# Attention and top-2 experts on one core: expert choice on logits, shorter routing, work moved between engines, row maxima 24 steps ahead

## The chip, the cores and the metric

The kernel runs on 1 core of a Trainium2 chip. The metric is device time in microseconds, the median of several runs. Kernel before: 1321.52 us, median of 3 runs (1320.3 to 1324.97).

## What is computed

x is 16 sequences of 512 tokens of 128 numbers, fp32. Attention has 16 heads of 8; V and U (8 x 32) work inside each head, and a softmax over 512 keys lies between. Then a layer norm, a layer of 8 experts of which each token uses two, and a second layer norm.

```python
zq, zk, zv = q @ V, k @ V, v @ V
att = softmax(einsum('bhqr,bhkr->bhqk', zq, zk) / sqrt(32))
x = layernorm(x + (att @ zv @ U.T) @ Wo.T + bo)
p = softmax(x @ gate_w.T)            # 8 experts
scores, idx = top_k(p, 2);  scores /= scores.sum()
out = sum over the two of score_e * (relu(x @ w1[e].T + b1[e]) @ w2[e].T + b2[e])
x = layernorm(x + out)
```

## The kernel before

**Attention, batch by batch.** A batch is one sequence. `schedule` writes out one body for each n from -2 to 17 on every engine, so that five stages overlap: while batch b has its softmax (`cur`), batch b+1 has its row maxima (`nxt`), batch b+2 is projected and split (`proj`), batch b-1 is finished up to its gate logits (`prev`), and batch b-2 gets its experts chosen, its places computed and its rows scattered (`prev2`). A body has 32 steps s. In a step TensorE (PE) makes one score tile for the exponentials (`scores`, L578, two matmuls), one for the maxima (`maxima`, L594), after every second step one product with the values (`av`, L556), and then what `misc(s)` asks for: every odd step may use the one spare PSUM bank `misc_ps`. ScalarE (ACT) takes the exponential of a 128 x 1024 tile (L687), VectorE (DVE) the maximum over such a tile (L853). Three PSUM tiles `score_ps` go round: `scores(s)` waits for the maximum of step s-2 (`red_done`), `maxima(s)` for the exponential of step s-1 (`exp_done`).

**Row maxima.** The negated maxima are needed in transposed form as extra rows of `q_stack`. After each 16 steps of maxima PE transposes them (`max_transpose`, at s = 23 for half 0 of b+1 and at s = 1 for half 1 of b), DVE negates (`neg`, L700, at s = 24 and 2), GpSimd (POOL) splits the fp32 numbers into three bf16 parts (`split_max`, four instructions), and SP issues six small DMAs (`max_rows`, L944), on which `scores(0)` and `scores(16)` wait.

**Expert choice.** For batch b-1 the logits appear at s = 27. `choose` is a chain of 21 small DVE instructions (k = 0 to 20), each waiting for the one ahead of it: it subtracts the largest logit, ACT takes the exponential (s = 30), and the softmax is finished before the two largest probabilities are found. k = 0 to 3 run at s = 28 and 31, the others in the first nine steps of the next body. PE counts the tokens of each expert at s = 17, `route` (k = 0 to 8, ten instructions) turns that into row numbers at s = 18 to 22, and POOL starts eight indirect DMAs (L923), one for each of 4 token tiles and 2 choices, in one run at the end of its body, behind `split_max(n1, 0)`.

**Queues.** POOL's order in a body: split_max(b,1), x + bias (L902), split_q, 1/sqrt of the variance (L908, L911), split_k, split_max(b+1,0), eight scatters. SP's order: x_in, last stack group of b+1, x_res, max_rows(b,1), store q parts, store k parts, max_rows(b+1,0), then stack groups 0, 1, 2 of b+2 (L956, 256 KB each).

**Start and end.** In body -1 there are 32 steps of maxima alone; from s = 16 on, every second step also transposes one expert's weights, which have been loaded into `probs`. After the last batch come the tail of its chain and then the expert stage (136 tiles of 128 rows, L1088 to L1236) and the second layer norm; the change touches neither.

Of the kernel before, what the change touches and what calls it, by code (L numbers as in the profile page):

```python
# [17 lines left out]
HALF = STEPS  # L18
POS = 8
# [7 lines left out]
TOP_STEPS = 19  # L27
# [8 lines left out]
SCALE_AT = 18  # L36
# [35 lines left out]
def build_layer(nc, x, wq, bq, wk, bk, wv, bv, wo, bo, u, v, gate_w, w1, b1, w2, b2, out):  # L72
# [19 lines left out]
    with top:  # L92
# [13 lines left out]
        bv_b = sb("bv_b", [P, P])  # L106
# [16 lines left out]
        with att:  # L123
# [31 lines left out]
            rstd = asb("rstd", [P, QT])  # L155
            shift = asb("shift", [P, QT])

            rows = [[asb(f"rows{n}_{w}", [P, QT, ROW]) for w in range(2)] for n in range(2)]
# [5 lines left out]
            top_logit = asb("top_logit", [P, QT])  # L164
            logits = asb("logits", [P, QT, E])
            exps = asb("exps", [P, QT, E])
            gate_sum = asb("gate_sum", [P, QT])
            gate_inv = asb("gate_inv", [P, QT])
            gate_p = asb("gate_p", [P, QT, E])
# [5 lines left out]
            chosen = [[asb(f"chosen{n}_{w}", [P, QT, E]) for w in range(2)] for n in range(2)]  # L175
            pair_sum = asb("pair_sum", [P, QT])
            pair_inv = asb("pair_inv", [P, QT])
            chosen_any = [asb(f"chosen_any{n}", [P, QT, E], bf16) for n in range(2)]
            slot = asb("slot", [P, QT, E])
            slot_of = asb("slot_of", [P, QT, E])  # L180
            slot_f = asb("slot_f", [P, 2, QT])
            slot_i = [asb(f"slot_i{n}", [P, 2, QT], i32) for n in range(2)]
            place_i = asb("place_i", [P, 2, QT], i32)
            place_f = asb("place_f", [P, 2, QT])
# [27 lines left out]
            bv_wide = asb("bv_wide", [P, P])  # L212

# [13 lines left out]
            pe_setup, dve_setup, place_ready = sem("pe_setup"), sem("dve_setup"), sem("place_ready")  # L227

            with nc.Block() as block:
# [28 lines left out]
                def _(pool):  # L258
# [40 lines left out]
                    nc.gpsimd.iota(place_i[:, :, :], pattern=[[1, 2], [2 * P, QT]], base=0, channel_multiplier=2).then_inc(place_ready, 1)  # L299
# [3 lines left out]
                def _(pe):  # L303
# [3 lines left out]
                    for n in range(2):  # L307
# [18 lines left out]
                    nc.tensor.matmul(score_ps[2][:, 0, P:2 * P], bv_wide[:, :], vhr, start=True, stop=True).then_inc(pe_setup, 1)  # L326
                    pe.wait_ge(dve_setup, 7)
                    nc.tensor.matmul(score_ps[2][:, 1, 0:P], u_hr[:, :, :].rearrange("p h r -> p (h r)"), wo_nt[:, :],
                                     start=True, stop=True).then_inc(pe_setup, 1)

                @block.vector
                def _(dve):
# [17 lines left out]
                    dve.wait_ge(place_ready, 2)  # L350
                    nc.vector.tensor_copy(tile_no[:, :], tile_no_i[:, :]).then_inc(dve_setup, 1)
                    nc.vector.memset(one_row[:, :], 1.0).then_inc(dve_setup, 1)
                    nc.vector.tensor_copy(place_f[:, :, :], place_i[:, :, :]).then_inc(dve_setup, 1)
                    nc.vector.memset(av_ps[:, :], 0.0).then_inc(dve_setup, 1)

# [58 lines left out]
            with nc.Block() as block:  # L414
                @block.tensor
                def _(pe):
                    def body(b, cur, nxt, proj, prev, prev2):
                        n1, n2, p1, p2 = b + 1, b + 2, b + -1, b + -2

                        def misc(s):  # L420

                            if s == 1 and cur:
                                wait(pe, S["red_done"], b.count(STEPS, STEPS))
                                if prev:
                                    wait(pe, S["yn_sb"], p1.count(HG, 3))
                                else:
                                    wait(pe, S["negmax_sb"], b.count(2, 1))
# [852 lines left out]
```

## Time and profile before

| | us |
|---|---|
| median of 3 runs | 1321.52 |
| the profiled execution's own time | 1309.61 |
| its span, first to last instruction | 1307.8 |
| first exponential starts | 84.4 |
| batches 0 and 1 (first exponential to the next batch's) | 48.0 and 48.2 |
| batches 2 to 14, 13 batches from 180.6 to 915.9 | 735.3 |
| batch 15 | 43.4 |
| last exponential's end to the expert stage's steady run | 43.2 |
| expert stage | 257.9 |
| final stage | 47.4 |

Read it as a chain of stages: batches are told apart by the start of their first exponential, which is a point in time common to all engines. Busy time of an engine is recorded from start to end of each instruction; ends of matmuls are modelled, so for PE what its semaphores release is the safer sign.

### The profile page before, as it was taken

To read this page: it belongs to the slowest core of one execution; us is meant where nothing else is said; L and a number is where in the kernel's file an instruction comes from. 1 tells how busy PE (TensorE), PEld (TensorE's weight loads), DVE (VectorE), ACT (ScalarE), POOL (GpSimd) and SP (SyncE) were. 2 spreads that over 40 slices of the span, in tenths; PEclk is the share of its full clock that TensorE was granted. 3 is DMA by queue.
4 is the path that set the end of the run, shared out by engine and by line. 5 is a ranking of instruction groups with operands and counts; after the bars stand their busy time and mean duration, and the time that the engine had idled before them with its cause. 6 is when DMAs were issued, how large, how long until landed. Compare 5 with 4: busy or idle time off the path is not lost. (4 is left out here: it accounts for less than half of the span.)

```text
span 1307.8 us, 24700 instructions
## 1 busy us (share of the span) xinstructions
PE 1072.2 (82%) x7709; PEld 508.8 (39%) x7709; DVE 1016.2 (78%) x2339; ACT 894.1 (68%) x1113; POOL 583.3 (45%) x780
## 2 busy tenths in 40 slices
PE   3478998879798887979788797977744999999977
PEld 1132222222122222213222222312224999999962
DVE  2588898879797887979779797978335888888855
ACT  1057887668586675858667675756844999999937
POOL 1123415344343533434443343523234777777745
PEclk9999999889898988989999898989986999999989
DMA  3832233341313324131342413220002222222236
GB/s 73 261 115 77 82 104 80 87 123 46 107 52 97 109 63 122 50 99 52 97 118 55 122 50 99 56 84 26 10 21 71 69 70 70 69 69 70 69 133 271
DMA packets 108790, 114.31 MB, mean 87 GB/s; under 512 B 19816, under 2 KB 82066, under 8 KB 108704
## 3 DMA queue, kind: packets, MB, share of 16 engines
q1 hardware_dynamic: 99104, 92.10, 25.0%
q0 software_dynamic: 8448, 16.93, 3.7%
q10 hardware_dynamic: 1152, 4.19, 0.8%
q8 instruction: 47, 0.77, 0.2%
q14 instruction: 39, 0.32, 0.1%
HBM read 64.45 MB, written 48.44 MB: 86 GB/s over the span
## 5 line engine op out<-in xcount | busy, mean ns | idle before, releaser
L853 DVE TENSOR_REDUCE row_max<-score_ps 128x2 f32<-128x1024 f32 x512 | 614.4, 1218 | 126.6 <-PE score_ps L594 69.2
L687 ACT ACTIVATE probs<-score_ps 128x1024 f32<-128x1024 f32 x512 | 519.7, 1024 | 223.5 <-PE score_ps L578 149.5
L556 PE MATMUL av_ps<-probs,v_one 128*9 128x512 f32 x2048 | 287.3, 635 | 9.8 <-ACT probs L687 9.1
L594 PE MATMUL score_ps<-k_stack,q_stack 64*128 64x512 bf16 x1024 | 209.7, 407 | 98.9 <-issue 48.8
L578 PE MATMUL score_ps<-q_stack,k_stack 64*128 64x512 bf16 x1024 | 207.7, 404 | 54.2 <-DVE row_max L853 49.4
L578 PEld LDWEIGHTS score_ps<-q_stack,k_stack 64*128 64x128 bf16 x1024 | 49.0, 93 | 355.5 <-DVE row_max L853 198.0
L1140 ACT ACTIVATE w_cur<-experts 128x1156 f32 x136 | 158.5, 1167 | 41.9 <-PEq L414 22.0
L1236 POOL DMA_INDIRECT y_d<-y_out,place x136 | 137.1, 1008 | 43.5 <-issue 43.5
L923 POOL DMA_INDIRECT routed_d<-rows,slot_i x128 | 125.1, 977 | 47.7 <-issue 39.3
L388 POOL TENSOR_TENSOR max_parts<-neg_max,zeros 32x128 bf16<-32x128 f32 x32 | 14.3, 446 | 295.0 <-DVE neg_max L700 295.0
L1097 PE MATMUL up_ps<-xt_sb,w_cur 128*128 128x128 f32 x1088 | 145.0, 277 | 0.0
L1105 PE MATMUL down_ps<-w_cur,hidden_r 128*128 128x128 f32 x1088 | 143.4, 275 | 0.0
L1097 PEld LDWEIGHTS up_ps<-xt_sb,w_cur 128*128 128x128 f32 x1088 | 133.6, 194 | 0.0
L1105 PEld LDWEIGHTS down_ps<-w_cur,hidden_r 128*128 128x128 f32 x1088 | 132.3, 192 | 0.0
L594 PEld LDWEIGHTS score_ps<-k_stack,q_stack 64*128 64x128 bf16 x1024 | 51.6, 95 | 152.3 <-issue 61.5
L388 POOL TENSOR_TENSOR q_parts<-q_f,zeros 128x512 bf16<-128x512 f32 x15 | 19.1, 1276 | 174.3 <-ACT q_f L664 174.3
L1194 DVE TENSOR_TENSOR hidden<-up_ps,w_cur 128x512 f32<-128x512 f32 x136 | 93.6, 688 | 2.2 <-PE up_ps L1097 2.0
L1148 ACT ACTIVATE hidden_r<-hidden 128x512 f32<-128x512 f32 x136 | 85.3, 627 | 5.8 <-DVE hidden L1194 5.1
L1231 POOL TENSOR_TENSOR half_x<-x_rows_sb,halves 128x128 f32<-128x128 f32 x136 | 53.6, 394 | 34.8 <-DVE y_out L1182 25.3
L556 PEld LDWEIGHTS av_ps<-probs,v_one 128*9 128x9 f32 x2048 | 30.6, 89 | 98.3 <-issue 87.6
L1178 DVE TENSOR_TENSOR y_bias<-down_ps,w_cur 128x128 f32<-128x128 f32 x136 | 39.7, 292 | 27.8 <-issue 24.5
L634 ACT ACTIVATE y_sb<-av_ps 128x512 f32<-128x512 f32 x64 | 38.2, 598 | 24.2 <-PE av_ps L556 24.2
(191 smaller groups left out, 1176.0 us busy)
## 6 DMA issues: line engine op xcount, KB each, us to landing
k_stack<-k_stack_d SPq DMA_DIRECT2D x64, 256.0 KB, 3.4
q_stack<-q_stack_d SPq DMA_DIRECT2D x64, 256.0 KB, 4.2
x_rows_sb<-routed_d SPq DMA_DIRECT2D x136, 65.0 KB
q_stack_d<-q_parts SPq DMA_DIRECT2D x32, 192.0 KB, 2.8
k_stack_d<-k_parts SPq DMA_DIRECT2D x32, 192.0 KB, 2.8
x_in<-L_attn_x SPq DMA_DIRECT2D x16, 256.0 KB, 6.4
q_stack_d<-q_parts SPq DMA_DIRECT2D x32, 128.0 KB, 2.5
k_stack_d<-k_parts SPq DMA_DIRECT2D x32, 128.0 KB, 2.6
```

The source lines that it names most:

```text
L556: last = nc.tensor.matmul(av_ps[32 * g:32 * g + V_COLS, :], v_one[n.parity][:, kb, HG * hg + g, :], probs[:, (2 * j + g // 2) % P_RING, g ...
L578: last = nc.tensor.matmul(score_ps[2 * s % 3][:, a, :], k_stack[b.parity][at, c, kb * P:(kb + 1) * P], q_stack[b.parity][at, c, :], start= ...
L594: last = nc.tensor.matmul(score_ps[(2 * s + 1) % 3 if cur else s % 2][:, a, :], q_stack[n1.parity][at, c, g * P:(g + 1) * P], k_stack[n1.p ...
L687: nc.scalar.activation(probs[:, s % P_RING, :, :], score_ps[2 * s % 3][:, :, :], ACT.Exp).then_inc(S["exp_done"], 1)
L853: nc.vector.tensor_reduce(row_max[:, s // (STEPS // 2), :, s % (STEPS // 2)], score_ps[(2 * s + 1) % 3 if cur else s % 2][:, :, :], AX.X, ...
L923: nc.gpsimd.indirect_dma_start(routed_d, bass.IndirectOffsetOnAxis(ap=slot_i[p2.parity][:, w, t:t + 1], axis=0), rows[p2.parity][w][:, t, ...
L1097: last = nc.tensor.matmul(up_ps[u % 4][:, h * P:(h + 1) * P], w_cur[u][:, h * P:(h + 1) * P], xt_sb[u % 2][:, :], start=True, stop=True)
L1105: last = nc.tensor.matmul(down_ps[u % 2][:, :], hidden_r[u % 4][:, h, :], w_cur[u][:, HID + h * D:HID + (h + 1) * D], start=(h == 0), stop ...
L1140: nc.scalar.activation(w_cur[u][:, :], experts[:, bass.ds(e, 1), :].rearrange("p a h -> p (a h)"), ACT.Copy).then_inc(M["w_copied"], 1)
L1148: nc.scalar.activation(hidden_r[u % 4][:, :, :], hidden[u % 4][:, :, :], ACT.Relu).then_inc(M["relu_out"], 1)
L1194: nc.vector.tensor_tensor(hidden[u % 4][:, :, :], up_ps[u % 4][:, :].rearrange("p (h t) -> p h t", t=P), w_cur[u][:, B1].unsqueeze(2).to_b ...
L1236: nc.gpsimd.indirect_dma_start(y_d, bass.IndirectOffsetOnAxis(ap=place[u][:, :], axis=0), y_out[u][:, :], None, bounds_check=2 * B * T - 1 ...
```

## The change

- `choose` works on the logits, which ACT now copies out of PSUM (s = 28): 16 instructions instead of 21. Of the softmax only exp(second - first) is taken (ACT, s = 2). They run at s = 29 to 31 and 0 to 4.
- `route` has 5 instructions instead of 10: both choices in one tensor; the places come from an `iota` on POOL. It runs at s = 6 to 8; PE's count moves from s = 17 to s = 5.
- The layer norm's shift moves from DVE to POOL (two small instructions), the negation of the maxima and the copy of the values from DVE to ACT. The value bias is multiplied with Wo once and added to bo in the setup.
- LAG: row maxima run 24 steps ahead of the exponentials instead of 32. Body -1 has 24 steps of maxima alone, and the last 24 steps of batch 15 have none. Half 0 of b+1 is now transposed at s = 25 (ACT negates at 26), half 1 of b at s = 9 (ACT at 10).
- POOL's eight scatters are started as 2 + 4 + 2, at three places of its order; split_q comes behind the variance.
- SP: stack groups 0 and 1 of b+2 now go ahead of max_rows(b+1,0).
- Most steps of `misc` change place; the wait for `misc_ps` is written as one function, `emptied`.

```diff
+LAG = 24
-TOP_STEPS = 19
+TOP_STEPS = 16
+SLOT_STEPS = 5
...
+            def maximum_at(b, s):
+                m = b.c * STEPS + s + LAG
+                return m if 0 <= m < B * STEPS else None
...
+            def max_bank(b, s):
+                return score_ps[s % 2] if b.c < 0 else score_ps[(2 * (b.c * STEPS + s) + 1) % 3]
...
+                            order = ((1, proj, "xt_sb", n2, 1, 1), (3, prev, "yn_sb", p1, HG, 4), (5, prev2, "slot_step", p2, SLOT_STEPS, 2),
+                                     (7, prev, "ynt_sb", p1, 1, 1), (9, cur, "negmax_sb", b, 2, 2), (11, prev, "res_ready", p1, 1, 1),
+                                     (13, proj, "q_sb", n2, 1, 1), (15, proj, "k_sb", n2, 1, 1), (17, cur, "yn_sb", b, HG, 1),
+                                     (19, nxt, "v_sb", n1, 1, 1), (21, cur, "yn_sb", b, HG, 2), (23, prev, "x1t_sb", p1, 1, 1),
+                                     (25, nxt, "negmax_sb", n1, 2, 1), (27, prev, "logits_sb", p1, 1, 1), (29, cur, "yn_sb", b, HG, 3))
...
+                            if s == 10 and cur:
+                                neg(b, 1)
+                            if s == 20 and nxt:
+                                act.wait_ge(S["v_done"], n1.count(1, 1))
...
+                            if s == 26 and nxt:
+                                neg(n1, 0)
+                            if s == 25 and prev:
                                 act.wait_ge(S["x1_ready"], p1.count(QT, QT))
...
+                            if s == 2 and prev2:
+                                act.wait_ge(S["top_step"], p2.count(TOP_STEPS, 8))
+                                nc.scalar.activation(second[:, :], best_gap[:, :], ACT.Exp).then_inc(S["second_sb"], 1)
...
-                            if s == SCALE_AT and prev:
-                                shift_out(p1)
...
+                            elif k == 2:
+                                step = nc.vector.tensor_tensor(slot_of[:, :, :, :], chosen[n.parity][:, :, :, :],
+                                                               slot[:, :, :].unsqueeze(1).to_broadcast([P, 2, QT, E]), ALU.mult)
+                            elif k == 3:
+                                step = nc.vector.tensor_reduce(slot_f[:, :, :], slot_of[:, :, :, :], AX.X, ALU.add)
...
+                        if prev2:
+                            pool.wait_ge(S["place_out"], p2.count(1, 1))
+                            pool.wait_ge(S["top_step"], p2.count(TOP_STEPS, TOP_STEPS))
+                            pool.wait_ge(S["slot_step"], p2.count(SLOT_STEPS, SLOT_STEPS))
+                            pool.wait_ge(S["copied"], p2.count(1, 1))
+                            scatter(p2, 0, 2)
...
                         if proj and not is_first(b):
+                            split_q(nc.gpsimd, pool, n2)
                             split_k(nc.gpsimd, pool, n2)
                         if prev2:
...
+                            scatter(p2, 2, 6)
                         if nxt:
                             split_max(n1, 0)
                         if prev2:
...
+                            scatter(p2, 6, 8)
...
+                            sp.wait_ge(S["parts_stored"], n2.count(16 * STORES, 16 * STORES))
+                            wait(sp, S["st_done"], b.count(STEPS, 2 * GROUP) if cur else 0)
+                            stacks(n2, 0)
+                            stacks(n2, 1)
                         if nxt:
                             max_rows(n1, 0)
```

## Rows read from the trace of the kernel before

**Rows 1.** The page: busy time by engine; granted TensorE clock in 40 slices (tenths).

```profile
PE 1072.2 (82%) x7709; PEld 508.8 (39%) x7709; DVE 1016.2 (78%) x2339; ACT 894.1 (68%) x1113; POOL 583.3 (45%) x780
PEclk9999999889898988989999898989986999999989
```

**Rows 2.** Windows: us; busy us (count) of PE, PEld, DVE, ACT, POOL; clock, DMA, GB/s.

```profile
132.40:180.60 48.20, 44.46 (x316) 13.46 (x314) 43.57 (x59) 38.66 (x48) 15.70 (x19) 1.00 0.31 87
...
180.60:235.70 55.10, 45.72 (x330) 13.81 (x328) 47.20 (x84) 39.00 (x48) 23.63 (x27) 0.94 0.38 105
...
462.40:519.80 57.40, 48.55 (x330) 13.98 (x328) 47.05 (x84) 38.90 (x47) 23.47 (x27) 0.89 0.30 86
...
915.90:959.30 43.40, 33.41 (x245) 9.47 (x242) 12.83 (x56) 36.26 (x44) 13.24 (x16) 0.97 0.05 14
959.30:1002.50 43.20, 10.17 (x76) 7.70 (x77) 19.15 (x83) 8.52 (x13) 18.42 (x20) 0.62 0.15 44
1002.50:1260.40 257.90, 257.22 (x2302) 257.02 (x2301) 221.07 (x810) 231.01 (x268) 187.68 (x268) 1.00 0.24 67
```

**Rows 3.** Windows inside batch 1 and batch 2: steps 0 to 27, steps 28 to 31.

```profile
132.40:174.10 41.70, 39.51 (x280) 12.19 (x278) 37.69 (x48) 33.92 (x42) 15.70 (x19) 1.00 0.26 72
174.10:180.60 6.50, 4.95 (x38) 1.27 (x36) 5.87 (x11) 4.73 (x7) 0.00 (x0) 1.00 0.65 183
180.60:223.30 42.70, 39.59 (x294) 12.43 (x292) 41.08 (x73) 34.25 (x41) 17.86 (x21) 1.00 0.25 74
223.30:235.70 12.40, 6.13 (x40) 1.38 (x36) 6.12 (x12) 4.76 (x7) 5.77 (x6) 0.72 0.80 213
```

**Rows 4.** Timeline, ScalarE, batch 7: exponentials of steps 28 and 29.

```profile
506.64 1.02 ACT L687 ACTIVATE probs<-score_ps 128x1024 f32<-128x1024 f32 x1 [0.50 <-issue]
512.78 1.02 ACT L687 ACTIVATE probs<-score_ps 128x1024 f32<-128x1024 f32 x1 [5.11 <-remote]
```

**Rows 5.** Timeline, TensorE and GpSimd, batch 7, around the same moment.

```profile
503.89 1.03 POOL L923 DMA_INDIRECT routed_d<-rows,slot_i  x1 [0.18 <-issue]
...
506.75 1.05 PE L556 MATMUL av_ps<-probs,v_one 128*9 128x512 f32 x8
...
508.85 0.39 PE L578 MATMUL score_ps<-q_stack,k_stack 64*128 64x512 bf16 x2
```

**Rows 6.** Timeline, batch 15: first scatter of eight; copy that waited for TensorE.

```profile
941.88 1.04 POOL L923 DMA_INDIRECT routed_d<-rows,slot_i  x1 [6.17 <-DVE rows L800]
...
951.75 0.60 ACT L674 ACTIVATE x_t<-misc_ps 128x512 f32<-128x512 f32 x1 [1.10 <-remote]
```

**Rows 7.** Groups by line: VectorE work that goes, with means of one (ns).

```profile
L829 DVE TENSOR_TENSOR v_one<-misc_ps,bv_b 128x512 f32<-128x512 f32 x16 | 10.9, 681 | 0.0
...
L700 DVE TENSOR_SCALAR neg_max<-misc_ps 32x128 f32<-32x128 f32 x32 | 8.6, 269 | 2.5 <-PE misc_ps L540 2.5
...
L728 DVE SCALAR_TENSOR_TENSOR shift<-mean_var,rstd 128x4 f32<-128x4 f32 x16 | 14.2, 886 | 1.2 <-POOL rstd L911 1.2
...
L743 DVE TENSOR_TENSOR logits<-misc_ps,top_logit 128x32 f32<-128x32 f32 x16 | 3.1, 191 | 0.6
```

**Rows 8.** Timeline, batch 1: negation of the maxima, issue of their six loads.

```profile
168.02 0.27 DVE L700 TENSOR_SCALAR neg_max<-misc_ps 32x128 f32<-32x128 f32 x1
...
170.36 4.14 SPq L944 DMA_DIRECT2D q_stack<-max_parts  x6
```

**Rows 9.** Source line L944: time to landing.

```profile
DMA to landing us min/median/max: 1.6/1.7/3.1
```

**Rows 10.** Windows at the start: expert weights still loading; from their first transpose on.

```profile
62.00:64.00 2.00, 2.00 (x4) 0.42 (x4) 1.48 (x2) 0.00 (x0) 0.00 (x0) 1.00 0.35 78
64.40:84.40 20.00, 15.58 (x107) 9.66 (x105) 19.08 (x18) 9.28 (x18) 6.59 (x8) 1.00 0.36 96
```

**Rows 11.** Timeline, GpSimd, behind the last batch: first and last of 16 scatters.

```profile
970.69 1.03 POOL L923 DMA_INDIRECT routed_d<-rows,slot_i  x1 [2.23 <-DVE rows L800]
...
993.24 0.96 POOL L923 DMA_INDIRECT routed_d<-rows,slot_i  x1 [0.30 <-issue]
```

More of the change, by code:

```diff
@@ L35 @@
 EXPERT_AT = [STEPS - 2 * (E - e) for e in range(E)]
-SCALE_AT = 18
+SCALE_AT = 16
+LEAST = -3.0e38
 class Batch:
@@ L155, in build_layer @@
             rstd = asb("rstd", [P, QT])
+            minus_mean = asb("minus_mean", [P, QT])
             shift = asb("shift", [P, QT])
-            rows = [[asb(f"rows{n}_{w}", [P, QT, ROW]) for w in range(2)] for n in range(2)]
+            rows = [asb(f"rows{n}", [P, 2, QT, ROW]) for n in range(2)]
             x1_t = asb("x1_t", [P, T])
@@ L329, in _ @@
                                      start=True, stop=True).then_inc(pe_setup, 1)
+                    pe.wait_ge(act_setup, 2)
+                    nc.tensor.matmul(misc_ps[:, 0:P], bv_hr[:, :], wo_t[:, :], start=True, stop=True).then_inc(pe_setup, 1)
                 @block.vector
@@ L807, in route @@
                             step.then_inc(S["slot_step"], 1)
                         for s in range(STEPS):
[L810 to L818 removed]
+                            if 29 <= s and prev:
+                                for k in (2 * s - 58, 2 * s - 57):
+                                    choose(p1, k)
@@ L819, in body @@
+                            if s <= 4 and prev2:
+                                for k in (2 * s + 6, 2 * s + 7):
+                                    choose(p2, k)
+                            if 6 <= s <= 8 and prev2:
+                                for k in (2 * s - 12, 2 * s - 11):
+                                    if k < SLOT_STEPS:
                                         route(p2, k)
@@ L895, in split_max, with scatter @@
                                   lambda k: n.count(6, 3 * half + k), S["maxsplit_done"])
-                        if cur:
-                            split_max(b, 1)
+                        def scatter(n, first, last):
+                            for k in range(first, last):
+                                w, t = divmod(k, QT)
+                                nc.gpsimd.indirect_dma_start(
+                                    routed_d, bass.IndirectOffsetOnAxis(ap=slot_i[n.parity][:, w, t:t + 1], axis=0),
+                                    rows[n.parity][:, w, t, :], None).then_inc(scattered[n.parity], 16)
+                        if prev2:
+                            wait(pool, scattered[p2.parity], p2.count_parity(8 * 16, 0))
+                            nc.gpsimd.iota(rows[p2.parity][:, :, :, D + 1].bitcast(i32), pattern=[[1, 2], [2 * P, QT]],
+                                           base=2 * T * p2.c, channel_multiplier=2).then_inc(S["place_out"], 1)
                         if prev:
@@ L903, in body @@
                                                     ALU.add).then_inc(S["xbo_ready"], 1)
-                        if proj and not is_first(b):
-                            split_q(nc.gpsimd, pool, n2)
+                        if cur:
+                            split_max(b, 1)
+                        if prev2:
+                            pool.wait_ge(S["place_out"], p2.count(1, 1))
[3 more added lines that the diff above has]
+                            scatter(p2, 0, 2)
                         if prev:
```

384 lines of the change are left out of this document (146 added, 238 removed).

## The prediction

> **What bounds the kernel now.** The page comes first: PE 82%, DVE 78%, ACT 68% busy, and a TensorE clock that falls to 8 tenths again and again in the first three quarters of the span [rows 1]. That is an average over stages, so the windows come next, cut at each batch's first exponential [rows 2]. The expert stage (257.9 us, PE busy 257.2) is bound by PE at full clock and is not touched. Attention is 875 us, and its batches differ: batch 1 takes 48.2 us, batch 2 55.1, batch 7 57.4; the 13 batches from 2 to 14 take 735.3, or 56.6 each. Batch 1 has no `prev2`, so it shows a batch without choice tail, routing and scatters.
>
> Where do the 8 us lie? I cut batches 1 and 2 at step 28 [rows 3]. Steps 0 to 27 take 41.7 against 42.7 us; steps 28 to 31 take 6.5 against 12.4. So 27 more small DVE instructions (3.4 us more of busy DVE, 37.7 to 41.1) cost 1.0 us, and four steps cost 5.9 us in which no engine is busier than before. In the timeline of batch 7 the exponential of step 28 starts at 506.64, the next at 512.78, after 5.11 us idle, released by something the view can't name [rows 4]. It waits for `scores(29)`. PE's records show its matmuls sent until 508.85 [rows 5], so PE had its instructions, yet what they release comes 4 to 5 us late: **the array pauses**. It happens in each of the batches 2 to 14 and not in 0 and 1, and about 3 us after the first of eight scatters (503.89 in batch 7) [rows 5]. After it the clock is low: 0.72 in the last four steps of batch 2, against 1.00 in batch 1 [rows 3], which adds about 1 us at the next batch's start (batch 7 as a whole: clock 0.89, 57.4 us [rows 2]). Batch 15 has the eight scatters with no SP transfers beside them: from 941.88 on, and only at 949.6 to 951.75 does PE lag, by some 2 us [rows 6]. So the pause goes with the run of scatters, and is longer where row maxima and stacks are loaded at the same time.
>
> **The change, part by part.** The sum is made against the profiled execution, 1309.6 us; the median of the runs lies 11.9 above it, and I add that at the end.
>
> *DVE work.* Gone in each batch: value copy 0.68, two negations 0.54, shift 0.89, five instructions of `choose` and five of `route` at 0.16 to 0.19 each [rows 7], 1.8 together: 3.9 us of record. DVE busy falls from 47.2 to about 43.4, which is what batch 1 has, 43.6 [rows 2]. By the two batches' first 28 steps, 3.4 us of busy DVE are worth 1.0 us [rows 3], since PE, ACT and DVE wait for one another through three PSUM tiles. So I take batch 1 as the **template: 48.2 us**. Ends: 47.2 and 49.2.
>
> *ACT work.* Added: value copy, two negations, logits copy, exp of the gap; gone: exps. The nearest rows are DVE's 0.68 and 0.27 for the same tiles [rows 7]: +1.3 us on an engine with 38.7 busy of 48.2. The cover is ACT's slack between exponentials; it is thinnest at s = 17 to 20, where scaling, a y copy and the value copy come together. On the path: 0 to 1.3, I take 0.3.
>
> *POOL.* iota, minus_mean and shift are some 0.2 us each. var_eps now comes ahead of split_q, which then ends near s = 18 and split_k near s = 22; both were waited for by stores with a whole batch of time. Hidden, 0.
>
> *Scatters 2 + 4 + 2.* Each costs POOL 0.96 and 0.30 between two [rows 11], as before. The first two start behind split_max at s = 10 to 12, four behind split_k at about s = 22, two behind split_max at s = 28. In batch 7 the pause began after the third scatter of a run, in batch 15 after the sixth. Pairs then stay below it; the four may just reach it. The price of what is left has ends 0 and 7.3 us per batch (5.9 from rows 3 plus 1.4 of low clock behind it). I take the case of batch 15, the nearest with few transfers beside it: a lag of 2 us, of which the three-tile ring hides some: 1.3.
>
> Here a page speaks against it. The Trainium skill (Trainium Architecture — The Big Picture, section What this means for kernel authors) says that the engine side and the DMA side of SBUF are physically separate and can't contend. If that were all, scatters could not hold PE and the pause would have another cause and stay; the trace doesn't agree so far, since the pause comes only in batches with scatters. It is a rival below.
>
> *Row maxima loads come later.* Half 1 was ready 14 steps ahead of `scores(16)`, half 0 8 steps ahead of `scores(0)`; now both have 6. From negation to landing: 168.29 (end) to 170.36, six issues in 4.14, then 1.7 [rows 8, 9], so 7.4 to 7.9 us; six steps are 6 x 41.7 / 28 = 8.9 us [rows 3], less 0.5 for the matmuls. Slack 0.5 to 1 us. Half 0 also stands behind two stack groups (1 MB) on SP. Behind `scores(0)` the whole of PE waits, and ACT and DVE behind it. Ends 0 and 3.1 - 1.7 + 2 = 3.4 (slowest landing, two more us for the stacks); I take 0.3.
>
> A middle batch after: 48.2 + 0.3 + 1.3 + 0.3 = 50.1; 13 of them 651, **84 us less** than 735.3. Batches 0 and 1 gain nothing and may wait: +1.
>
> *LAG.* Body -1 has 8 steps less (20.0 us for 16 steps [rows 10], so 10 us), but the weights' loading stands in the way: the DMA share is down to 0.35 only from 62 us [rows 10], and the weight transposes can't start before. From their first to the first exponential it is 20.0 us [rows 10], paced by PE and ACT with one PSUM tile. So the first exponential comes at about 82 instead of 84.4: -2 (ends -3.4 and 0). Batch 15 gets 8 steps with maxima: +0.5. No more of the 10 us is won.
>
> *Behind the last batch.* The 16 scatters run from 970.69 to 994.2 [rows 11] and end the 43.2 us window [rows 2]. Two can start earlier and the last batch's slots come about ten small instructions earlier: -1.3 (ends -3 and 0). The setup's added product is hidden by SP's blank rows.
>
> **Sum:** -84 + 1 - 2 + 0.5 - 1.3 = -86; 1309.6 - 86 = 1223.8; plus 11.9: **1236 us**.
>
> **The rivals.**
> - *A, as summed:* pause short or gone. With nothing left of it and template 47.2: 1236 - 13 x 2.6 = 1202. With 2 us more in each batch: 1262.
> - *B, the pause is halved:* the run of four and the pair at s = 28, which stands beside max_rows and two stack groups, each still stop PE for one of the shorter times. 3 to 4 us per batch instead of 1.3: 1258 to 1290 with some lateness of the row loads. For it: the middle batches have SP transfers beside every group.
> - *C, the pause stays:* its cause isn't the run of scatters (the page's rule above), or the last pair is enough. Then only DVE's 1 us per batch and start and tail remain: 13 x 1.0 + 3 less, so 1305; with lateness 1320. Against: batches 0 and 1. This is also the case where the change doesn't do what it says, since shorter chains on DVE alone are worth little.
> - *D, slower:* every group, however short, stops PE once. One stop costs 7.3 us now; three at half of that are 11: 13 x (11 - 7.3) = +48, less the 16 us of C: 1354. It decides from the point at which the three groups together cost more than 7.3 + 1.2 us per batch. Against: the expert stage has one scatter in every 1.9 us, and PE is busy 257.2 of 257.9 [rows 2].
>
> **How the numbers follow.** A 0.55, B 0.21, C 0.16, D 0.08. About 0.3% (4 us) is what a measurement of this kernel can tell from no change. A and B are faster, of C two thirds, D slower: faster 0.86, same 0.06, slower 0.08. The range from 1204 to 1308 takes in the bounds of A and B and half of C.
>
> **What would show it.** Right: windows of batches 2 to 14 at 49 to 51 us with clock near 1.00; no exponential more than 3 us behind the one ahead; DVE busy 43 to 44 per batch; first exponential at 82. If the pause shows behind the group of four only, A or B; behind `max_rows` at s = 28 still 5 us, C. If `scores(0)` and `scores(16)` wait for a DMA of `q_stack<-max_parts`, the six-step distance was too short. The prediction would be wrong by most if the pause hangs on something that both kernels have, as the row loads at s = 26 to 28.

## The result, and the profile after

The changed kernel takes **1256.89 us** (median of 4 runs, 1254.57 to 1261.33) beside 1322.94 for the kernel before: ratio 0.951, 95% interval 0.947 to 0.954. The profiled execution took 1257.83, its span is 1255.7.

The page of the changed kernel, the two lines that answer to [rows 1]:

```profile
PE 1064.8 (85%) x7711; PEld 515.8 (41%) x7711; DVE 972.6 (77%) x2115; ACT 904.7 (72%) x1177; POOL 588.2 (47%) x827
...
PEclk9989999899999999988999889899958999999989
```

The same kernel's windows, cut at the same events as [rows 2] (first line: start; then batch 0, batch 1, batches 2 to 14, batch 15, tail, expert stage; columns as there):

```profile
0.00:83.20 83.20, 38.41 (x164) 20.31 (x166) 35.82 (x45) 15.73 (x33) 17.49 (x63) 0.95 0.54 158
83.20:133.40 50.20, 42.27 (x278) 10.37 (x274) 39.60 (x38) 35.44 (x41) 14.40 (x17) 0.92 0.30 87
133.40:182.20 48.80, 44.66 (x314) 13.34 (x314) 42.37 (x56) 39.35 (x52) 15.99 (x22) 1.00 0.31 88
182.20:863.40 681.20, 605.79 (x4258) 183.91 (x4258) 579.53 (x911) 513.65 (x661) 300.55 (x382) 0.96 0.31 88
863.40:908.00 44.60, 34.45 (x261) 10.00 (x259) 18.44 (x54) 36.52 (x46) 12.46 (x18) 1.00 0.04 13
908.00:950.40 42.40, 11.29 (x79) 8.78 (x80) 16.66 (x64) 8.80 (x17) 18.62 (x23) 0.57 0.15 46
950.40:1208.30 257.90, 257.08 (x2299) 256.87 (x2298) 219.83 (x809) 231.20 (x268) 187.41 (x268) 1.00 0.24 67
```

| stage | before | after | difference | forecast |
|---|---|---|---|---|
| first exponential | 84.4 | 83.2 | -1.2 | -2 |
| batches 0 and 1 | 96.2 | 99.0 | +2.8 | +1 |
| batches 2 to 14 | 735.3 (56.6 each) | 681.2 (52.4 each) | -54.1 | -84 |
| batch 15 | 43.4 | 44.6 | +1.2 | +0.5 |
| tail | 43.2 | 42.4 | -0.8 | -1.3 |
| profiled span | 1307.8 | 1255.7 | -52.1 | -86 |

The medians lie 66 us apart and the profiled executions 52, so some 14 us of the gain are in no trace.

All of the gain that the traces show is in the middle batches, and there it comes out of the pause. Clock there is 0.96 where the kernel before had 0.92 over 180.6 to 915.9. What is left of the pause stands behind the third and fourth of the four scatters that follow split_k. Timeline of the changed kernel, batch 4: GpSimd's four scatters, SyncE's stores of the k parts beside them, and what ScalarE and VectorE wait for (start, us, engine, operation, idle before it and its releaser):

```profile
321.12 4.24 SPq L920 DMA_DIRECT2D k_stack_d<-k_parts  x6
321.26 1.03 POOL L855 DMA_INDIRECT routed_d<-rows,slot_i  x1 [0.17 <-issue]
...
323.60 1.03 ACT L694 ACTIVATE probs<-score_ps 128x1024 f32<-128x1024 f32 x1
...
325.11 0.96 POOL L855 DMA_INDIRECT routed_d<-rows,slot_i  x1 [0.30 <-issue]
325.21 0.10 PEld L530 LDWEIGHTS misc_ps<-ident,row_max 128*32 128x32 f32 x1 [0.42 <-issue]
...
326.54 0.60 ACT L623 ACTIVATE y_sb<-av_ps 128x512 f32<-128x512 f32 x1 [1.39 <-remote]
327.27 1.02 ACT L694 ACTIVATE probs<-score_ps 128x1024 f32<-128x1024 f32 x1
327.31 1.23 DVE L808 TENSOR_REDUCE row_max<-score_ps 128x2 f32<-128x1024 f32 x1 [2.28 <-remote]
```

It is the picture of [rows 4, 5], smaller: TensorE's instructions are sent until 325.4, but what they release comes some 2 us late, and both waiting engines name "remote" (the releaser that the view can't name). From the exponential of step 24 (323.60) to the next are 3.67 us; in batch 1, without scatters, that step takes 1.90. Batches 2 to 13 all show it at step 24 (3.6 to 4.4 us); in batches 2, 8, 9, 11, 12 and 13 the granted clock falls to its lower level behind it and steps 26 to 28 take up to 3 us each. Batch 14, which doesn't, has four scatters in a row too, but no stores beside them: 48.5 us. The pairs at steps 12 and 28 show no stop.

A small wait is new. PE transposes x for batch b+2 at step 1, where it was step 5, and SyncE issues the load of `x_in` at the head of its turn, behind stack loads. Waits of the changed kernel (in total, times, longest):

```profile
PEld misc_ps L457 <- DMA x_in<-L_attn_x: 14.2, 9, 2.8
...
PE misc_ps L457 <- DMA x_in<-L_attn_x: 9.7, 8, 2.3
```

In the kernel before no such wait shows: from batch 1 on x_in was issued 3 to 9 us before the first exponential of a batch and used 7.4 to 9.1 us after it. Now it is issued 1 to 6 us before and wanted at about 1.7 after.

### The profile page after: what moved, and what is told of

Same layout as the page of the kernel before. It is cut to its first block and busy times, and to the rows that moved or that the text cites. A ratio compares the mean times of both kernels' runs of the same rounds, so it can differ in the third digit from the quotient of the medians.

```text
span 1255.7 us, 24651 instructions
## 1 busy us (share of the span) xinstructions
PE 1064.8 (85%) x7711; PEld 515.8 (41%) x7711; DVE 972.6 (77%) x2115; ACT 904.7 (72%) x1177; POOL 588.2 (47%) x827
## 5 line engine op out<-in xcount | busy, mean ns | idle before, releaser
L808 DVE TENSOR_REDUCE row_max<-score_ps 128x2 f32<-128x1024 f32 x512 | 617.9, 1220 | 134.6 <-PE score_ps L583 94.0
L546 PE MATMUL av_ps<-probs,v_one 128*9 128x512 f32 x2048 | 277.8, 615 | 8.2 <-ACT probs L694 6.4
L583 PE MATMUL score_ps<-k_stack,q_stack 64*128 64x512 bf16 x1024 | 204.0, 396 | 74.6 <-ACT probs L694 55.6
L565 PE MATMUL score_ps<-q_stack,k_stack 64*128 64x512 bf16 x1024 | 204.0, 396 | 24.2 <-DVE row_max L808 19.0
L1109 ACT ACTIVATE w_cur<-experts 128x1156 f32 x136 | 158.5, 1167 | 36.5 <-PEq L425 17.2
L565 PEld LDWEIGHTS score_ps<-q_stack,k_stack 64*128 64x128 bf16 x1024 | 49.2, 93 | 315.1 <-issue 156.6
L1205 POOL DMA_INDIRECT y_d<-y_out,place x136 | 136.8, 1006 | 43.4 <-issue 43.4
L1057 PE MATMUL xt_ps<-ident,x_rows_sb 128*128 128x128 f32 x136 | 37.8, 278 | 18.0 <-DMA x_rows_sb<-routed_d 18.0
```

Of the source, the lines that this page charges most:

```text
L546: last = nc.tensor.matmul(av_ps[32 * g:32 * g + V_COLS, :], v_one[n.parity][:, kb, HG * hg + g, :], probs[:, (2 * j + g // 2) % P_RING, g ...
L565: last = nc.tensor.matmul(exp_bank(b, s)[:, a, :], k_stack[b.parity][at, c, kb * P:(kb + 1) * P], q_stack[b.parity][at, c, :], start=True, ...
L583: last = nc.tensor.matmul(max_bank(b, s)[:, a, :], q_stack[n.parity][at, c, g * P:(g + 1) * P], k_stack[n.parity][at, c, :], start=True, s ...
L808: nc.vector.tensor_reduce(row_max[:, m // (STEPS // 2), :, m % (STEPS // 2)], max_bank(b, s)[:, :, :], AX.X, ALU.max).then_inc(S["red_done ...
L1109: nc.scalar.activation(w_cur[u][:, :], experts[:, bass.ds(e, 1), :].rearrange("p a h -> p (a h)"), ACT.Copy).then_inc(M["w_copied"], 1)
L1205: nc.gpsimd.indirect_dma_start(y_d, bass.IndirectOffsetOnAxis(ap=place[u][:, :], axis=0), y_out[u][:, :], None, bounds_check=2 * B * T - 1 ...
```

## The experiments

Twelve runs in four sets, ten of edited kernels and one each of the changed kernel and the kernel before again; each set shares a chip and runs of the kernel before. **The chips differ, and that became the main finding.** Chip A (first set): the kernel before takes 1323.2 us (19 runs), as in the pair above, whose chip is not on record. Chip B (second and third set): 1220.0 and 1216.8 us. Chip C (fourth set): 1218.3 us. So the ratios to the kernel before are what can be compared inside a set; across sets only traces of like chips.

For reference, here are the windows from batch 2's first exponential to batch 15's (13 batches) in all kernels, one line each; they are used below. Where a step's mean is given, it is over batches 3 to 13. Chip A, in the order eight in one run, SyncE's order undone, four ahead of the splits, four opened up:

```profile
183.60:910.10 726.50, 609.79 (x4256) 181.20 (x4256) 585.00 (x911) 510.76 (x660) 300.56 (x382) 0.93 0.30 83
```

```profile
192.20:904.70 712.50, 627.56 (x4260) 189.68 (x4258) 577.91 (x911) 513.98 (x661) 301.26 (x382) 0.93 0.30 86
```

```profile
192.60:918.70 726.10, 605.71 (x4258) 181.82 (x4258) 585.91 (x911) 511.87 (x661) 301.40 (x382) 0.94 0.29 84
```

```profile
193.60:904.40 710.80, 603.09 (x4258) 180.77 (x4258) 587.25 (x911) 511.23 (x661) 302.73 (x382) 0.95 0.30 86
```

### Eight scatters in one run again (chip A)

```diff
-                            scatter(p2, 0, 2)
...
-                            scatter(p2, 2, 6)
...
-                            scatter(p2, 6, 8)
+                            scatter(p2, 0, 8)
```

> Changed kernel with one part undone: all eight x-row scatters of a batch are issued in one run behind the first V split of the next batch, as in the kernel before. Theory (the pause of PE comes from a long run of scatters beside other transfers): in the changed kernel step 24 of batches 2 to 13 has a gap between exponentials of 3.6 to 4.4 us against 1.9 without scatters; with a run of eight the pause is as long as in the kernel before and sits at steps 28 to 29, each middle batch grows from 52.4 us to about 55 (half of the way back to 56.6), the whole 1285 to 1305 us. Rival (how the scatters are grouped doesn't matter, the gain came from the shortened DVE work and the value copy): 1257 us, within 4, with middle batches of 52 to 53.

**1313.94 us**, ratio 0.994 (0.991 to 0.997) where the changed kernel had 0.951. Middle batches 726.5 / 13 = 55.9 us. Timeline of ScalarE, batch 4 (the run of eight starts at 336.71):

```profile
339.68 1.02 ACT L694 ACTIVATE probs<-score_ps 128x1024 f32<-128x1024 f32 x1 [0.96 <-PE score_ps L565]
344.19 1.02 ACT L694 ACTIVATE probs<-score_ps 128x1024 f32<-128x1024 f32 x1 [3.48 <-remote]
348.54 1.94 ACT L694 ACTIVATE probs<-score_ps 128x1024 f32<-128x1024 f32 x2 [3.33 <-PE score_ps L565]
```

The pause is back: steps 29 and 30 take 3.7 and 5.4 us in the mean instead of 1.1 and 1.7, and the whole lies 9 us above what I expected. The rival, that the grouping doesn't matter, is out. With the split of the scatters undone, 0.6% is left of 4.9%: everything else in the change, shorter chains on VectorE, LAG and the moves between engines, is worth under 10 us here.

### SyncE's order undone (chip A)

```diff
+                        if nxt:
+                            max_rows(n1, 0)
                         if proj:
                             sp.wait_ge(S["parts_stored"], n2.count(16 * STORES, 16 * STORES))
                             wait(sp, S["st_done"], b.count(STEPS, 2 * GROUP) if cur else 0)
                             stacks(n2, 0)
                             stacks(n2, 1)
-                        if nxt:
-                            max_rows(n1, 0)
```

> Changed kernel with one part undone: SyncE issues the maximum rows of the next batch ahead of its wait for the stored q and k parts and of the stack loads 0 and 1, as in the kernel before. If late row loads cost what the prediction put them at (0.3 us in each of 14 batches), the whole falls by 2 to 5 us to about 1253; if the row loads have slack in the changed kernel (no wait of PE on them stands in its trace in the middle batches), the time stays within 2 us of 1257. The pause at step 24 stays either way. It is also the control of the next two.

**1303.75 us**, ratio 0.987 (0.984 to 0.989). Both numbers expected were wrong, by 45 to 51 us: the order that I had priced as a loss of 0.3 us per batch protects most of the gain. The waits of this kernel say why:

```profile
PEld misc_ps L457 <- DMA x_in<-L_attn_x: 39.2, 12, 6.3
...
PE misc_ps L457 <- DMA x_in<-L_attn_x: 33.4, 11, 5.8
```

Stack loads 0 and 1 now start behind max_rows(b+1,0), 2 to 7 us before the next batch's first exponential instead of some 10, so six stack loads stand right ahead of x_in on SyncE's queue and not two. In batches 0, 1 and 2 it is issued 0.3 to 1.1 us after the batch's first exponential and used 6 to 7 us after its issue; step 1 takes 6.6 to 8.3 us, and the clock is low after such a stop. The row maxima loads, the thing I had tested for, are waited for twice, 4.0 us in all, ahead of batch 0 and in batch 15, and just so in the changed kernel.

The late x_in is not all of it. Batches 0 to 14 take 41.5 us more than in the changed kernel: 29.5 at steps 0 to 6, where x_in is waited for, and 11.3 at steps 26 to 31. There the low clock follows the stop at step 24 in 11 of 12 batches and not in 6. Why it does so more often, no run tells.

### Four scatters where no stores run, and four one at a time (chip A)

Both with SyncE's order undone, so the run above is their control.

```diff
+                        if prev2:
+                            scatter(p2, 2, 6)
                         if proj and not is_first(b):
                             split_q(nc.gpsimd, pool, n2)
                             split_k(nc.gpsimd, pool, n2)
-                        if prev2:
-                            scatter(p2, 2, 6)
```

> The run with SyncE's order undone, and the four scatters 2 to 5 issued ahead of the q split instead of behind the k split, so that no q or k part is stored while they run. Theory 1 (the four stop PE only while SyncE's stores of parts run beside them, as batch 14 with four scatters and no stores took 48.5 us): the pause goes, middle batches 49 to 50, whole 1210 to 1225 us. Theory 2 (four scatters in a row stop PE whatever runs beside): the pause stays, at step 16 or 17 instead of 24, middle batches 52 to 53, whole 1250 to 1262 us.

```diff
-                            split_q(nc.gpsimd, pool, n2)
-                            split_k(nc.gpsimd, pool, n2)
+                            split_q(nc.gpsimd, pool, n2, one(2))
+                            if prev2:
+                                scatter(p2, 3, 4)
+                            split_k(nc.gpsimd, pool, n2, one(4))
+                            if prev2:
+                                scatter(p2, 5, 6)
```

> The run with SyncE's order undone, and the run of four opened up: scatter 2 inside the q split, 3 between the splits, 4 inside the k split, 5 behind it; so one at a time, with SyncE's stores of parts beside them. Theory 2 (the length of the run decides): the pause goes, middle batches 49 to 50, whole 1210 to 1225 us. Theory 1 (scatters beside stores are enough, one or four): the pause is spread out or stays, each batch 51 to 53, whole 1240 to 1262 us.

**1319.04 us** (0.998, 0.996 to 0.999) and **1297.76 us** (0.981, 0.977 to 0.984). By the total both theories fail. By the trace both edits did what they were made for: in both, step 24 takes 1.90 us in the mean, against 3.83 in the control, and nothing stops PE at steps 16 to 20 either. (With one at a time, step 28 takes 2.0 to 2.3 us instead of 1.5 in nine of twelve batches, behind the last pair and beside the row loads; by the end of step 31 that is made up.) Windows over steps 24 to 28 of a middle batch, first the changed kernel (batch 4), then the four ahead of the splits (batch 4):

```profile
323.60:333.12 9.52, 7.00 (x55) 2.07 (x53) 6.25 (x7) 6.47 (x11) 5.79 (x10) 1.00 0.68 205
```

```profile
348.40:356.18 7.78, 7.00 (x55) 2.07 (x53) 6.25 (x7) 6.22 (x11) 6.65 (x11) 1.00 0.67 183
```

So on chip A the four stopped PE only where they came in a row **and** beside the stores; either half alone did not. What ate the gain is x_in. The splits end some 5 us later (four scatters at 1.27), with them the stores, the stack loads and x_in behind them. Waits of the first, then of the second:

```profile
PE misc_ps L457 <- DMA x_in<-L_attn_x: 83.3, 14, 6.9
```

```profile
PE misc_ps L459 <- DMA x_in<-L_attn_x: 72.1, 14, 7.0
```

Step 1 takes 7.9 and 6.6 us in the mean, step 2 2.6 and 2.5 (low clock).

### x_in loaded half a batch earlier (chip B)

```diff
-                        if proj and not is_first(b) and not is_first(p1):
-                            wait(sp, S["xt_done"], b.count(1, 1))
-                            sp.dma_start(x_in[n2.parity][:, :, :], tokens(x_rows, n2)).then_inc(x_loaded[n2.parity], 16)
...
                         if cur:
                             max_rows(b, 1)
+                        if 2 <= n3.c < B:
+                            wait(sp, S["xt_done"], n1.count(1, 1))
+                            sp.dma_start(x_in[n3.parity][:, :, :], tokens(x_rows, n3)).then_inc(x_loaded[n3.parity], 16)
```

> Changed kernel with one more edit: SyncE issues the load of x_in for a batch right behind the second half's maximum rows of the batch before, some 25 us earlier, instead of at the head of its next turn behind the stack loads. The runs so far point to a wait that the prediction did not have: LAG 24 moved the x transposes of PE from step 5 to step 1, and the x_in load lands for them just in time or late (step 1 and 2 of batch 0: 4.5 and 2.8 us; batches 7 and 8: over 3 us). Theory (x_in wait): batch 0 falls from 50.2 to about 48 or less, batches 7 and 8 lose 1 to 2 us each, whole 1247 to 1254 us. Rival (the slow first steps come from something else): 1257, within 3.

> The run with SyncE's order undone (1303.8 us), with x_in loaded early as in the run beside it. Theory (all of the 47 us that SyncE's order is worth is the x_in load, queued behind six stack loads instead of two): the waits at step 1 go, the whole falls to that of the run beside it, 1245 to 1256 us. Rival (late stack loads or maximum rows themselves hold PE up): it stays above 1285 us.

> SyncE's order as in the changed kernel, x_in loaded early, and the four scatters 2 to 5 ahead of the q split. In the run of the four ahead of the split the pause at step 24 was gone (step 24 took 1.90 us in the mean, as in batch 1, against 3.82), and all that it gained and more was lost to the wait for x_in (step 1: 7.87 us). Theory: with both, the middle batches take 48.5 to 49.5 us and the whole 1203 to 1218 us. Rival (something else takes the place of the x_in wait, such as the stack loads that start 5 us later): 1235 us or more.

> SyncE's order as in the changed kernel, x_in loaded early, and the four scatters issued one at a time between the operations of the q and k splits. As before, theory: pause gone and no wait for x_in, whole 1203 to 1218 us, within 4 us of the run beside it; the splits end about 5 us later in both. Rival: 1235 us or more.

Here the kernel before took 1220.0 us. The times: x_in early **1214.66** (ratio 0.996, 0.994 to 0.998); with SyncE's order undone besides **1211.79** (0.994, 0.992 to 0.996); four ahead of the splits **1271.21** (1.042, 1.038 to 1.047); one at a time **1254.1** (1.028, 1.023 to 1.033). The absolute numbers were expected for a chip like A and can't be compared here. For the last two the rival was right, though: something else took the place of the wait for x_in, and both are slower than the kernel before. Windows over batches 2 to 14 in the same order:

```profile
180.30:821.90 641.60, 585.24 (x4258) 178.67 (x4258) 584.17 (x911) 510.95 (x661) 300.61 (x382) 0.99 0.32 93
```

```profile
179.60:817.90 638.30, 582.02 (x4258) 177.69 (x4258) 583.49 (x911) 510.62 (x660) 300.52 (x382) 1.00 0.33 95
```

```profile
178.80:878.30 699.50, 606.73 (x4258) 181.14 (x4258) 588.43 (x911) 511.68 (x662) 301.41 (x382) 0.95 0.29 85
```

```profile
178.80:861.30 682.50, 604.01 (x4258) 180.87 (x4258) 588.47 (x911) 511.84 (x661) 302.65 (x382) 0.96 0.30 88
```

Three things follow. First, with x_in early no wait for it is left in any of the four, and SyncE's new order protects nothing any more: it costs 0.3 us a batch (49.4 against 49.1), 2.9 us in the whole. The waits for the row loads show it, first with the new order, then with the old:

```profile
PE score_ps L565 <- DMA q_stack<-max_parts: 14.9, 8, 3.5
```

```profile
PE score_ps L565 <- DMA q_stack<-max_parts: 4.0, 2, 3.5
```

The six waits more are all ahead of `scores(0)` of a middle batch, 1.5 to 2.5 us each. So on this chip the new order has nothing to protect but x_in. On chip A, where it was worth 47 us, x_in early was not run, and what of the 11 us behind the pause would be left there is open. Second, the first two still have four scatters in a row beside the stores, and step 24 takes 1.90 us in both: on this chip **the pause doesn't occur at all**. Third, the last two show the cost of SyncE's new order at its largest. Waits, first four ahead of the splits, then one at a time:

```profile
PE score_ps L565 <- DMA q_stack<-max_parts: 65.5, 14, 5.7
```

```profile
PE score_ps L567 <- DMA q_stack<-max_parts: 51.2, 14, 4.5
```

The row loads of half 0 stand there behind SyncE's wait for the stored parts; once the splits end 5 us later, the row loads miss `scores(0)`, and steps 31 and 0 take 5.9 and 2.8 us.

### The changed kernel again, and a combination meant for both kinds of chip (chip B)

> The changed kernel itself, as control. The kernel before took 1323 us beside one set of runs and 1220 us beside the other, which is a chip on which the pause seems not to occur (with x_in early and a run of four beside the stores, step 24 took 1.90 us). If on this run's chip the kernel before takes about 1320: 1257 us, within 4. If it takes about 1220: the theory that the gain was almost wholly the shortened pause expects 1213 to 1222 us (ratio 0.995 to 1.003); the rival, that shortened DVE work and better order are worth most of the gain everywhere, expects a ratio of 0.97 or less.

> x_in loaded early, the four scatters ahead of the q split, and SyncE's order as before the change. The same with the changed kernel's SyncE order took 1271 us, because PE waited 50.3 us for late maximum rows, which stand there behind SyncE's wait for the stored parts. Theory (that wait was all): no wait on maximum rows, middle batches 48.5 to 49.5 us, 1203 to 1215 us on either chip, since no run of four stands beside stores. Rival: the pause comes back on a chip where the kernel before takes 1320 us: 1235 us or more there.

Kernel before 1216.8 us. The changed kernel: **1231.49 us, ratio 1.013 (1.007 to 1.018)**, 1.3% slower; its four runs spread from 1226 to 1238. Neither ratio expected (0.995 to 1.003, or 0.97 and less) came true, since neither had the wait for x_in in it. x_in early, four ahead of the splits and SyncE's order as before the change: **1213.65** (0.997, 0.995 to 0.999), as expected, but for two waits for row loads in middle batches (1.8 and 2.0 us). It is no faster than the run with x_in early and that order alone (0.994): without the pause, moving the four gains nothing. Windows of the changed kernel on this chip, batch 0 and batches 2 to 14, and then batches 2 to 14 of the combination:

```profile
82.80:133.10 50.30, 41.73 (x278) 10.29 (x274) 39.70 (x38) 35.47 (x41) 14.43 (x17) 0.92 0.31 88
...
181.80:831.90 650.10, 586.09 (x4258) 177.76 (x4258) 585.64 (x911) 512.28 (x660) 301.28 (x382) 0.99 0.32 92
```

```profile
181.20:820.80 639.60, 583.49 (x4258) 178.16 (x4258) 583.68 (x911) 510.76 (x661) 301.43 (x382) 1.00 0.32 95
```

The same moment as above, the same kernel, the other chip (timeline, batch 4, the four scatters at 317.07 to 321.89 and the stores of k from 316.93 on):

```profile
319.40 1.03 ACT L694 ACTIVATE probs<-score_ps 128x1024 f32<-128x1024 f32 x1
...
320.83 0.61 ACT L623 ACTIVATE y_sb<-av_ps 128x512 f32<-128x512 f32 x1
321.31 1.05 ACT L694 ACTIVATE probs<-score_ps 128x1024 f32<-128x1024 f32 x1
```

Up to the fourth scatter the two timelines agree to 0.02 us from instruction to instruction (the last two exponentials lie 1.39 us apart in both, the scatters 1.33, 1.26 or 1.27, and 1.26); then here the next exponential comes after 1.91 us and there after 3.67. The instructions are the same, so the pause comes with the chip, or with what else happened on it; which, no run can tell. The wait for x_in is larger here, since the batches are shorter: 17.2 us in 13 times for PE. This is what made the loss: with x_in early the kernel is 17 us faster by the medians (1231.49 against 1214.66) and 21 by the ratios to the kernel before (1.013 and 0.996). Of that the two profiled executions show 11, 2.6 in batch 0 and 8.5 in batches 2 to 14.

### The kernel before on a chip without the pause, and more work for VectorE (chip C)

> The kernel before itself, for its trace on this run's chip. If its time is about 1220: the theory (no pause on that chip) expects steps 28 and 29 of its middle batches to take about what they take in batch 1, the middle batches 48.5 to 49.5 us and the granted clock above 0.97; the rival (the pause is there and something else is faster) expects them still at 55 to 57 with a shorter time elsewhere. If its time is about 1320: the trace shown before the prediction again.

1220.19 us, clock 0.971. The window over its batch 4, then over batches 2 to 14:

```profile
282.93:332.20 49.27, 44.59 (x330) 13.70 (x328) 47.02 (x84) 38.97 (x47) 23.47 (x28) 1.00 0.33 95
```

```profile
182.40:828.60 646.20, 582.72 (x4260) 177.54 (x4262) 610.55 (x1093) 505.31 (x609) 294.95 (x343) 0.99 0.32 93
```

Eight scatters in one run, six row loads and the stack loads beside them, as in [rows 2, 3]; steps 28 and 29 take 1.51 and 1.13 us in the mean where the trace shown ahead of the prediction has 5.5 and 3.2. The theory holds: no pause, and 49.7 us a batch, 0.2 above what was expected.

```diff
+                            if cur and s < 27:
+                                nc.vector.tensor_tensor(pad_out[s][:, :, :], prefer[:, :, :], prefer[:, :, :], ALU.mult)
```

> The run with x_in early, the four scatters ahead of the q split and SyncE's order as before the change (1213.7 us beside 1216.8 of the kernel before), with 27 more VectorE instructions of 128x32 in each batch, one in each of steps 0 to 26, some 3.4 us of VectorE work a batch. The prediction put 3.4 us less of such work at 1.0 us a batch; by that this is 15 to 16 us slower, 1229 us. Rival (VectorE's work is hidden in most steps, the share that the limit takes is nearer nothing): 1214 to 1219 us. Second rival (it is on the path in every step): 48 us or more slower. On a chip where the kernel before takes 1320 us it should show no pause at step 24 either, and so stay below 1235 us there as well.

**1227.91 us**, ratio 1.008 (1.006 to 1.011) against 0.997 without the additions (on chip B), which is 14 us where 15 to 16 were expected. Batches 2 to 14 with them:

```profile
180.50:831.60 651.10, 580.59 (x4258) 176.91 (x4258) 640.71 (x1262) 515.68 (x660) 302.50 (x382) 1.00 0.32 94
```

50.1 against 49.2 us a batch, with 57.0 / 13 = 4.4 us more VectorE work (I had planned 3.4): 0.2 us for each microsecond of work, spread thinly over the steps. Both rivals are out, and the prediction's price for such work is near. What stays open: no kernel with x_in early was run on a chip with the pause, so the combination's worth there is not measured.

## Why the prediction was right or wrong

The forecast was 1236 us with a range of 1204 to 1308; 1256.9 lies in it and the sign is right. The working was right in less than that suggests.

**What bounds it: right, with a condition that the profile could not show.** The 8 us of a middle batch were read as a pause tied to the scatters. Undoing the split alone brings it back (0.951 to 0.994), so it is shown that on a chip like A the run of scatters brings the pause; what in it holds PE is not. But I took it for a property of the kernel. On chips B and C the same kernel has 49.7 us a batch instead of 56.6, and then the change has nothing to remove. The forecast has no case for that: on such a chip it would have given a gain of 86 us where there is a loss of 15.

**Scatters 2 + 4 + 2: mechanism right, size too small.** "The four may just reach it": they do, and the pairs don't. I took 1.3 us a batch for what is left. Like chips compared, it is 52.4 - 50.0 = 2.4 (the changed kernel on both), and what there was is 56.6 - 49.7 = 6.9 (I had 7.3). Under-sized by 1.1 x 13 = 14 us. The middle batches missed by 30 (681 against 651); of the rest x_in is 0.7 a batch (50.0 against 49.4 with it early) and the template 0.6 (49.1 with the old order of the row loads, where 48.5 was summed). Step 24 itself is 1.9 us longer, and steps 26 to 28, at low clock in six batches, 1.6 in the mean, of which some comes back in shorter waits later; my 1.3 held no low clock at all. The comparison with batch 15 was read half: I named the missing transfers, then took its 2 us for a place where stores run beside. Batch 14 of the changed kernel, four scatters and no stores, shows what the right use of that batch was.

**The page's rule.** The traces of chip A show a TensorE that has its instructions and releases late beside a run of scatters with transfers; those of chips B and C show no such thing. The rule that the engine side and the DMA side can't contend (the Trainium skill, Trainium Architecture — The Big Picture, section What this means for kernel authors) agrees with chips B and C, down to 1.91 us at step 24. On chip A something holds PE that the transfers bring on; whether it is SBUF was not tested, so no run here refutes the rule. The releaser is "remote".

**DVE work: size about right, bookkeeping not.** Without pause and with x_in early a middle batch takes 49.4 us, and 49.1 with the old order of the row loads; the kernel before takes 49.7. I had 48.8 and 48.5 against 49.2. So the moves between engines and the shorter chains are worth 0.6 us a batch all told, where 0.7 was summed. (The prediction counts 27 small instructions more in batch 2; the trace has 25.) But VectorE's busy time went from 47.0 to 45.0 us a batch (610.6 and 585.6 over 13, chips C and B; 47.2 to 44.6 on chip A) and not to 43.4. One reason stands in the rows. The shift cost VectorE 0.89 in the mean [rows 7], but 1.13 us where GpSimd ran a split beside it (0.15 elsewhere). Moved to GpSimd it is gone, yet in the changed kernel another small instruction meets GpSimd's x + bias. Timeline, batch 3 of the changed kernel:

```profile
282.08 1.29 POOL L866 TENSOR_TENSOR x_bo<-x_res,bo_b 128x512 f32<-128x512 f32 x1
282.24 1.19 DVE L740 TENSOR_TENSOR tied<-logits,best 128x32 f32<-128x32 f32 x1
```

Its twin elsewhere takes 0.18. It ends with GpSimd's instruction, to 0.06 us. So of the 3.9 us that I let go, 1.0 came back under another name in such a batch; there are 7 in this trace, and on chip B it is each of 13. That agrees with the Trainium skill (GPSIMD Engine Reference, section 1. Specifications), by which GpSimd shares its way to SBUF with VectorE instructions that have two inputs there; I had the rows for it and counted the 0.89 as work of the instruction. The rate itself, 1.0 us for 3.4 us of small work [rows 3], is near what the added instructions cost, 0.9 for 4.4.

**Row maxima loads: size right. SyncE's order: half of it missed.** I asked what comes later when max_rows moves behind the stack loads and found the row loads. 0.3 us a batch were set for them. In the changed kernel's middle batches no wait on them shows, but with x_in early the order costs 0.3 on chip B. I did not ask what comes earlier by that, nor where `misc(1)` had come from. The x transposes moved from step 5 to step 1, four steps (6 us) less of distance for x_in, which stands behind everything on SyncE's queue. PE's waits for it add up to 9.7 us in the changed kernel's profile and to 17.2 on chip B; with the old order they are 33.4 us on chip A, and the whole is 47 us longer. "Most steps of misc change place" stood in my own account of the change, and I costed none of them. This is the step that failed, and on chip B it turned the sign: 1.013, and 0.996 with x_in early.

**Start, batches 0 and 1, batch 15, tail.** -1.2, +2.8, +1.2 and -0.8 against -2, +1, +0.5 and -1.3: right in kind, small. Batch 0's +2.2 is x_in again (the transposes wait 2.08 us at 86.97).

**The 11.9 us between profiled execution and median: wrong.** I carried it over. The changed kernel's median lies 0.9 us below its profiled execution. So the sum missed by 34 us (-86 against -52) and the offset gave 13 back, with the medians 66 apart: the forecast was 21 us off by two errors of opposite sign.

**Chances.** A had 0.55 with 1202 to 1262, and the time is in it; by mechanism it is between A and B (the run of four still stops PE, the pair at step 28 doesn't). D, slower, had 0.08 by a mechanism that no run shows: no pair cost a batch any time. Slower came true on another chip by one I had not named.

## What to carry to other kernels

When a load's consumer moves forward by some steps, follow the load back through its queue and list what is issued ahead of it: the change of an order that looks like a loss for one transfer may be what another lives on, and the right cure is to issue the endangered load early, not to balance the queue (17 us here, and the old order became the better one by 3). A stop that no engine, semaphore or queue in the trace explains may belong to the chip: before building on its removal, look at the unchanged kernel on a second chip. And take a slow small VectorE instruction beside a GpSimd one for GpSimd's time: moving it moves the wait.

## What the runs showed of the hardware

- The same kernel took 1323 us on one chip and 1217 to 1220 on two others. The profiled executions lie 89 us apart, all of it in the 13 middle batches: 6.9 us each, for the pause and the low clock behind it.
- On the first chip, four scatters in a row beside stores from SBUF stopped TensorE for about 2 us (step 24: 3.8 us instead of 1.9). Four in a row without them didn't, nor did four beside them that start 3.6 to 3.8 us apart (1.90 both). Eight beside row and stack loads cost 7 us with the low clock. Pairs cost nothing in the changed kernel; in one run step 28 behind a pair was 0.5 to 0.8 us longer, and made up three steps later.
- Where a late x_in stretched step 1 to 5.7 us or more, the granted clock was at its lower level (1.2 GHz) for part or all of step 2, 0.50 to 0.72 in the mean, and step 2 took 2.1 to 2.8 us instead of 1.3.
- A VectorE instruction of 128x32 elements took 1.19 us instead of 0.18 beside a GpSimd addition of 1.29 us, and ended with it.
